# Attention units with sums on VectorE, four probability buffers and longer lags, in a four-layer fused kernel

## What is computed

```python
# layer 0: relative positions, head size 64, values of size 16
content = einsum('bind,bjnd->bnij', q + r_w_bias * SCALE, k)
pos = rel_shift_gather(einsum('bind,tnd->bnit', q + r_r_bias * SCALE, r_head), s, shift=1)
prob = softmax(content + pos, axis=-1)
# layer 1: head size 16, values of size 16
attn = softmax(einsum('bqhd,bkhd->bhqk', q, k) * scale, axis=-1)
# layer 2: head size 64, values of size 64
attn = softmax(einsum('bhnd,bhmd->bhnm', q, k) / SCALE, axis=-1)
# each: attn @ v, then a projection to 192 features, added to the residual
```

## Time and profile before

| | |
|---|---|
| median of three runs | 2116.0 us (2085.26, 2116.0, 2117.72) |
| profiled execution | 2114.3 us, of which the span from first to last instruction is 2112.6 us |
| mean granted TensorE clock | 0.787 of 2.4 GHz |
| TensorE, busy | 1645.4 us (78% of the span) |
| weight loads (PEld), beside it | 1202.3 us (57%) |
| ScalarE, busy | 706.5 us (33%) |
| VectorE, busy | 687.7 us (33%) |
| GpSimd, busy | 382.9 us (18%) |

### The profile page before, as it was taken

How to read it: one execution, slowest core, us unless ns; L and a number is a source line. 1 busy time by engine, 2 the same in 40 slices (tenths; PEclk the granted TensorE clock), 3 DMA queues, 4 the chain that set the end, 5 groups by cost and what they waited for, 6 DMA issues and landing times.

```text
span 2112.6 us, 31289 instructions
## 1 busy us (share of the span) xinstructions
PE 1645.4 (78%) x9952; PEld 1202.3 (57%) x9952; DVE 687.7 (33%) x2153; ACT 706.5 (33%) x2243; POOL 382.9 (18%) x450
## 2 busy tenths in 40 slices
PE   6888788875544557777878869958987899869994
PEld 4565656554322334555556758836656676668883
DVE  1233324245111116634343342224334323451112
ACT  0555454541100003366664201124445443203331
POOL 4111101011000002222220015512112100012331
PEclk9566656565677776888899759979899999858997
DMA  6122222223699983000000425420000020124553
GB/s 179 48 67 57 57 57 57 57 57 90 168 279 286 286 260 97 1 1 0 0 0 0 112 70 167 149 55 1 0 0 0 0 90 0 32 74 124 156 152 83
DMA packets 85963, 177.80 MB, mean 84 GB/s; under 512 B 34602, under 2 KB 53200, under 8 KB 83832
## 3 DMA queue, kind: packets, MB, share of 16 engines
q1 hardware_dynamic: 71344, 127.50, 21.9%
q10 hardware_dynamic: 7392, 33.03, 5.3%
q0 software_dynamic: 7136, 16.10, 2.6%
HBM read 149.61 MB, written 26.99 MB: 84 GB/s over the span
## 4 chain that ended last, share of the span: by engine, by line
PE 46%; issue 22%; DMA 17%; DVE 6%; ACT 5%; POOL 3%; SPq 1%; POOLq 0%; DVEq 0%; ACTq 0%
PE bank L1538 13%; DMA AREA<-in_fc 9%; PE bank L1968 5%; PE bank L1956 5%; PE bank L1715 4%; PE bank L1958 3%; PE bank L1707 3%; DMA pos_scratch<-AREA 3%; DMA AREA<-pos_scratch 2%; PE bank L1638 2%; PE bank L1769 2%; PE bank L1625 2%; PE bank L1648 1%; PE bank L1924 1%; DMA WM<-rows_out 1%
## 5 line engine op out<-in xcount | busy, mean ns | idle before, releaser
L1538 PE MATMUL bank<-XT,AREA 96*128 96x408 f32 (+1 forms) x640 | 244.9, 542 | 32.3 <-ACT XT L1320 15.0
L1538 PEld LDWEIGHTS bank<-XT,AREA 96*128 96x128 f32 (+1 forms) x640 | 124.5, 200 | 142.3 <-issue 103.4
L1625 PE MATMUL bank<-KZ,QT 128*102 128x102 f32 x1152 | 176.0, 305 | 20.6 <-ACT PB L1360 17.9
L609 POOL TENSOR_TENSOR PB<-PB,RCU 102x306 f32<-102x306 f32 x132 | 91.9, 696 | 534.3 <-DVE RCU L843 534.3
L1625 PEld LDWEIGHTS bank<-KZ,QT 128*102 128x102 f32 x1152 | 160.1, 219 | 31.7 <-ACT PB L1360 20.3
L1638 PE MATMUL bank<-PT,V 102*32 102x102 f32 (+1 forms) x1152 | 98.0, 302 | 82.2 <-ACT PT L1366 81.8
L595 POOL TENSOR_TENSOR RS<-VE,expo 102x4 f32<-102x4 f32 (+1 forms) x53 | 53.0, 1000 | 430.3 <-DVE VE L781 372.5
L1360 ACT ACTIVATE PB<-bank,NMU 102x102 f32<-102x102 f32 x264 | 88.0, 346 | 98.5 <-DVE NMU L837 97.5
L1968 PE MATMUL bank<-WM,KZ 128*128 x660 | 120.8, 332 | 0.0
L1956 PE MATMUL bank<-KZ,SLOTS 128*128 128x128 f32 x660 | 116.2, 301 | 2.5 <-issue 2.5
L1638 PEld LDWEIGHTS bank<-PT,V 102*32 102x32 f32 (+1 forms) x1152 | 48.2, 130 | 117.6 <-ACT PT L1366 61.7
(11 more groups left out here) (292 smaller groups left out, 2761.3 us busy)
## 6 DMA issues: line engine op xcount, KB each, us to landing
WM<-in_fc SPq DMA_DIRECT2D x9, 2304.0 KB, 22.4
AREA<-in_fc SPq DMA_DIRECT2D x9, 2304.0 KB, 17.9
WM<-in_fc ACTq DMA_DIRECT2D x7, 2304.0 KB, 29.2
AREA<-in_fc ACTq DMA_DIRECT2D x7, 2304.0 KB, 29.0
pos_scratch<-AREA SPq DMA_DIRECT2D x16, 913.5 KB
SLOTS<-in_m3w SPq DMA_DIRECT2D x33, 384.0 KB
SLOTS<-in_m1w SPq DMA_DIRECT2D x33, 256.0 KB
AREA<-pos_scratch SPq DMA_DIRECT2D x16, 459.0 KB
```

Of the source, the lines that this page charges most:

```text
L609: pool.tensor_tensor(p, p, scale, ALU.mult).then_inc(sem["probs_ready"], 1)
L1538: last = pe.matmul(dst, lhsT, rhs, start=n == 0, stop=n == len(pieces) - 1)
L1625: last = pe.matmul(psum[k][0:T, cols(j)], q, kk, start=True, stop=True)
```

## The change

- **Sums on VectorE.** The exponentials no longer use the accumulator; VectorE reduces each unit's exponentials from PB into SMU, ahead of the reciprocal.
- **Sign and scale in Q's copy.** ScalarE's copies of Q (and QR) are scaled by -0.125 or -0.25, and their biases are scaled once beforehand, so the scores arrive negative and scaled. VectorE takes the minimum and gives it as the exponential's bias, with scale -1; the instruction that multiplied the maxima (L837) goes.
- **Four buffers.** PB has a fourth buffer (in ON0), and MXU, SMU and RCU four places.
- **Banks.** In layers 1 and 2 the scores have three banks and the values two; in layer 0 two and one, as before. Banks of scores and values are freed through exp_ready and a new semaphore pair, values_ready and values_taken.
- **Lags on TensorE.** Turns are three steps behind the scores (before: two), values five (three). A projection comes in three parts in three steps, the first six steps after the batch row's last unit plus one, and is ahead of the values in its step; at the end all three parts stand in the last step.
- **Order on VectorE and ScalarE.** VectorE's copy of the values and the residual addition now stand behind the minimum and the sum of their step. ScalarE's copy of the turned unit (now s-4) stands ahead of the exponentials.
- **Positions in layer 0.** PR exists twice. The six pairs of batch row 2 are made two at a time in steps 0, 1 and 2, those of row 3 in steps 4, 5 and 6.

The core of the diff:

```diff
+POS_STEPS = (0, 1, 2, 4, 5, 6)
-        PB.append(ON[1][:, 0:4 * T].rearrange("p (h t) -> p h t", h=4))
+        for j in (1, 0):
+            PB.append(ON[j][:, 0:4 * T].rearrange("p (h t) -> p h t", h=4))
-        PR = a0(T, HEADS, NREL)
+        PR = [a0(T, HEADS, NREL),
+              SLOTS[0:T, NB * D:NB * D + HEADS * NREL].rearrange("p (h n) -> p h n", h=HEADS)]
-        STEPS = UNITS + 5
-        AVBANK, PROJBANK = OBANKS
+        STEPS = UNITS + 7
+        PROJBANK = OBANKS[1]
+        SCORES, VALUES = (SBANKS + XBANKS[:1], SBANKS), (OBANKS[:1] + XBANKS[1:], OBANKS[:1])
+        def proj_step(bb, i):
+            return min(UPB * bb + UPB + 6 + i, STEPS - 1)
# VectorE
-                step(dve.tensor_reduce(MX[:, 0:HPU], scores, AX.X, ALU.max))
-                give(ts(NMU[:, n % 3, 0:HPU], MX[:, 0:HPU], -scale, None, ALU.mult), "probs_in")
+                give(dve.tensor_reduce(MXU[:, n % 4, 0:HPU], scores, AX.X, ALU.min), "probs_in")
             def inverse_sums(n):
                 dve.wait_ge(sem["exp_ready"], at.take("exp_ready"))
-                give(dve.reciprocal(RCU[:, n % 3, 0:HPU], SMU[:, n % 3, 0:HPU]), "sums_ready")
+                step(dve.tensor_reduce(SMU[:, n % 4, 0:HPU], PB[n % 4][:, 0:HPU, :], AX.X, ALU.add))
+                give(dve.reciprocal(RCU[:, n % 4, 0:HPU], SMU[:, n % 4, 0:HPU]), "sums_ready")
+            def attention(dv, pos, finish):
+                for s in range(STEPS + 1):
                     if s < UNITS:
+                        minima(s, pos)
                     if 0 <= s - 1 < UNITS:
                         inverse_sums(s - 1)
+                    n = s - 6
+                    if 0 <= n < UNITS and av_filled(dv, n % UPB):
+                        tile, k = 3 * av_place(dv, HPU * (n % UPB))[3], VALUES[pos][fill_of(dv, n) % len(VALUES[pos])]
+                        dve.wait_ge(sem["values_ready"], at.take("values_ready"))
+                        src = psum[k][:, 0:3 * T].rearrange("p (k t) -> p k t", k=3)
+                        give(dve.tensor_copy(OT[n // UPB % 2][:, tile:tile + 3, :], src), "values_taken")
+                        dve.wait_ge(sem["values_taken"], at.now("values_taken"))
+                    for bb in range(GB):
+                        if s - 1 == proj_step(bb, 2):
+                            finish(bb, full(PROJBANK)[0:T, 0:D], PROJBANK)
# ScalarE
+                for s in range(UNITS + 4):
+                    if 0 <= s - 4 < UNITS:
                         k = at.bank(TBANKS)
                         src = full(k)[0:T, 0:TU].rearrange("p (h t) -> p h t", h=HPU)
                         free(activation(PT[s % 2][:, 0:HPU, :], src, ACT.Copy), k)
-                            last = activation(p, p if pos else psum[k][0:T, cols(j)], ACT.Exp, scale=scale,
-                                              bias=NMU[:, s % 3, j:j + 1], accum_out=SMU[:, s % 3, j:j + 1])
+                            last = activation(p, p if pos else psum[k][0:T, cols(j)], ACT.Exp, scale=-1.0,
+                                              bias=MXU[:, s % 4, j:j + 1])
-                    activation(QT[:, p, :], src, ACT.Identity, bias=rw0[:, p:p + 1])
-                    free(activation(QR[:, p, :], src, ACT.Identity, bias=rr0[:, p:p + 1]), k)
+                    activation(QT[:, p, :], src, ACT.Identity, scale=-0.125, bias=rw0[:, p:p + 1])
+                    free(activation(QR[:, p, :], src, ACT.Identity, scale=-0.125, bias=rr0[:, p:p + 1]), k)
# TensorE
-                        k = at.bank(SBANKS)
-                        if s < 2:
+                        k = banks[s % len(banks)]
+                        if s < len(banks):
+                    for bb in range(GB):
+                        for i in range(3):
+                            if s != proj_step(bb, i):
+                                continue
+                            if i == 0:
+                                taken(fills(dv) * (bb + 1) - 1)
+                                k, p = claim(None, PROJBANK)
+                            for m in range(i * parts // 3, (i + 1) * parts // 3):
+                                last = pe.matmul(psum[PROJBANK][0:T, 0:D], OT[bb % 2][:, m, :], wo[:, m, :],
+                                                 start=m == 0, stop=m == parts - 1)
-                    n = s - 3
+                    n = s - 5
-                            claim(None, AVBANK)
+                        if f >= len(places) and (unit == 0 or av_filled(dv, unit - 1)):
+                            taken(f - len(places))
-                    n = s - 2
+                    n = s - 3
-                    if pos and s in (UPB, 2 * UPB):
-                        pos(2 if s == UPB else 3)
+                    if pos and s in POS_STEPS:
+                        pos(2 + POS_STEPS.index(s) // 3, 2 * (POS_STEPS.index(s) % 3), 2)
```

More of the change, by code:

```diff
@@ L940, in _ @@
             dve.wait_ge(sem["w0_loaded"], W0_LOADS)
+            for w in (rw0, rr0):
+                give(ts(w, w, -0.125, None, ALU.mult), "scaled")
             def prepare_a0(g):
@@ L1060, in attend_1 @@
                 values(V, 16, bv1)
-                attention(16, False, 0.25, lambda bb, o, k: free(tt(a_of(g)(bb), a_of(g)(bb), o, ALU.add), k))
+                attention(16, False, lambda bb, o, k: free(tt(a_of(g)(bb), a_of(g)(bb), o, ALU.add), k))
             def prepare_f1(g):
@@ L1246, in attend_2 @@
                 values(V, 64, None)
-                attention(64, False, 0.125, lambda bb, o, k: free(tt(h_of(g)(bb), h_of(g)(bb), o, ALU.add), k))
+                attention(64, False, lambda bb, o, k: free(tt(h_of(g)(bb), h_of(g)(bb), o, ALU.add), k))
             def mlp_2(g):
@@ L1351, in exponentials, with attention @@
                 give(activation(buf, buf, ACT.Exp, scale=scale), name)
-            def attention(scale, pos=None):
-                for s in range(STEPS):
-                    if s < UNITS:
-                        k = at.bank(SBANKS)
-                        act.wait_ge(sem["probs_in"], at.take("probs_in"))
-                        for j in range(HPU):
-                            p = PB[s % 3][:, j, :]
-                            last = activation(p, p if pos else psum[k][0:T, cols(j)], ACT.Exp, scale=scale,
-                                              bias=NMU[:, s % 3, j:j + 1], accum_out=SMU[:, s % 3, j:j + 1])
-                        give(last, "exp_ready")
-                    if 0 <= s - 2 < UNITS:
+            def attention(pos=None):
+                for s in range(UNITS + 4):
+                    if 0 <= s - 4 < UNITS:
                         k = at.bank(TBANKS)
@@ L1454, in _ @@
                     k = at.bank(XBANKS)
-                    free(activation(QT[:, dst, :], full(k)[:, 0:TG], ACT.Identity, bias=bqk1[:, dst:dst + 1]), k)
+                    free(activation(QT[:, dst, :], full(k)[:, 0:TG], ACT.Identity, scale=-0.25,
+                                    bias=bqk1[:, dst:dst + 1]), k)
                 for j in range(3):
@@ L1484, in _ @@
                     k = at.bank(XBANKS)
-                    free(activation(QT[:, p, :], full(k)[:, 0:TG], ACT.Copy), k)
+                    free(activation(QT[:, p, :], full(k)[:, 0:TG], ACT.Copy, scale=-0.125), k)
                 for p in range(6):
@@ L1606, in mlp, with attention, taken @@
                     filled(last, k)
-            def attention(dk, per_tile, dv, wo, v_moved, pos=None, whole=False):
-                pt_moved, o_moved = {}, {}
+            def attention(per_tile, dv, wo, v_moved, pos=None):
+                pt_moved = {}
+                banks, places = SCORES[bool(pos)], VALUES[bool(pos)]
+                before = at.now("values_taken")
+                parts = 3 if dv == 16 else 6
+                def taken(f):
+                    pe.wait_ge(sem["values_taken"], before + f + 1)
                 for s in range(STEPS):
@@ L1637, in attention @@
                             row, rows, tile, _ = av_place(dv, h)
-                            last = pe.matmul(psum[AVBANK][row:row + rows, cols(tile)],
+                            last = pe.matmul(psum[k][row:row + rows, cols(tile)],
                                              by_head(dv)[:, bb * HEADS + h, :], PT[n % 2][:, j, :],
@@ L1647, in attention @@
                         for j in range(HPU):
-                            last = pe.transpose(p[0:T, cols(j)], PB[n % 3][:, j, :], ident[0:T, 0:T])
+                            last = pe.transpose(p[0:T, cols(j)], PB[n % 4][:, j, :], ident[0:T, 0:T])
                         pt_moved[n] = filled(last, k)
-                    if pos and s in (UPB, 2 * UPB):
-                        pos(2 if s == UPB else 3)
-                    bb = last_of(s - 4)
-                    if bb is not None:
-                        moved(o_moved[bb])
-                        k, p = claim(None, PROJBANK)
-                        filled(product(p[0:T, 0:D], [(OT[bb % 2][:, n, :], wo[:, n, :])
```

(10 more changed lines are left out.)

92 lines of the change are left out of this document (47 added, 45 removed).

## The result

The median of four executions fell from 2116.9 to 1974.3 us: a ratio of 0.9375, with a 95% interval of 0.9329 to 0.942. The prediction was 1997 us in a range of 1955 to 2060, so it held, and the time forecast was 23 us too high. The profiled execution took 1975.6 us (span 1973.8); the span is 138.8 us shorter.

The account below looks back on a forecast made before the run. Waits between engines, none full, were taken to bound the attention stretches, with TensorE's half clock costing most in layer 0. Layer sums -51, -30 and -36 gave -117 from 2114.3: 1997 us, range 1955 to 2060.

Parts of the forecast that it names:

- Layers 1 and 2: Attention stretches: TensorE's steady waits go, pace 1.25 and 1.44; -30 (bounds -23, -37) and -36 us (-27, -45).
- The wait for VectorE's copy ahead of a projection: TensorE waits for a copy queued behind minimum and sum: 0.7 us in layer 1, 0.5 in layer 2, two times.
- Half the stretches at half clock: Layers 1 and 2: half the stretches lose time to half clock, 3.5 us each in layer 1, 4.4 in layer 2.
- rival 1: All stretches: the clock holds at 2.4 GHz since TensorE has fewer gaps; -63 - 37 - 45, 1969 us; chance 0.17.
- Rivals 3 and 4: 3: VectorE serialises, 2118 us, chance 0.08. 4: TensorE stays at 1.2 GHz in layers 1 and 2, 2209, 0.05.
- Layer 0: Attention stretches: positions spread over steps, VectorE then paces at 1.73; 63.7 to 51 us each, -51 (bounds -63, -27).
- the wait of the values for the one value bank: Layer 0: TensorE's values idle about 2.4 us per batch row behind VectorE's later copy; two waits cost 4.0 before unit 15.
- SyncE's floor: Layer 0: position store 5.66 and load 4.69, 10.4 us per batch row; rows land at 11.4, 21.8, 32.2.
- Rival 2: Layer 0 gives nothing: value-bank wait, SyncE's chain and half clock eat the smoothed position blocks; 2048 us; chance 0.15.
- The accumulators: ScalarE: three accumulator reads go, -0.28 us per unit, a gain only in chains; keeps ScalarE from pacing layer 1 at 1.47.

Follow-up runs that it names:

- the fill in layers 1 and 2: The kernel before, with six extra float32 matmuls (results unused) after the scores of step 1 in layers 1 and 2; ratio 0.9899.
- position blocks: The kernel after, with the positions of batch rows 2 and 3 again as one block each, two PR kept; ratio 0.9637.
- the one with both edits: The kernel after, with VectorE's copy of the values first in its step and the sums back in ScalarE's accumulator; 1925.8 us, ratio 0.9169.

## Why the prediction was right, step by step

**Layers 1 and 2 (forecast -30 and -36, measured -29.3 and -36.2): the sums are right by two errors against each other.** The steady pace is exactly the floors of the earlier trace rows, 1.25 and 1.44, and the turns' wait in the head came as forecast (first turns 3.81 us after the first scores, 890.20 to 894.01; forecast 3.8). Two terms were mis-sized.
- *The wait for VectorE's copy ahead of a projection* was 0.7 in layer 1 and 0.5 in layer 2, and measured 1.42 (step of 3.00 against 1.58) and 1.2 (3.25 against 2.09). The term assumed that VectorE stands at the same step as TensorE. It runs a unit behind: its minimum at 901.90 is of the scores that started at 900.62, when those of 901.87 were already running, and sum, reciprocal and a gap put the copy 1.3 us behind that minimum. The second of the two waits, as long (steps of 3.03 and 3.36), was for the residual addition behind the copy, which the term did not hold. So unit 15's scores started at 22.1 and 25.0 us, not at 20.6 and 23.6, and the tails were 9.0 and 11.9 against 8.3 and 10.9: stretches of 31.1 and 36.9 against 28.9 and 34.5 at full clock.
- *Half the stretches at half clock* (+3.5 and +4.4 in them) did not happen; all ran at 1.00, as rival 1 said. That is 7 and 9 us too much in a layer, and the longer waits and tails were 8 and 9 too little (123.6 against 4 x 28.9, 146.9 against 4 x 34.5).

Rival 1's mechanism thus came true in these layers without its time, since its own sum held the same 0.7 and the same tails. That the layer sums fit to a microsecond is luck. Rivals 3 and 4 did not occur: the sum on VectorE found its exponentials done in nearly every step (0.5 and 0.6 us idle ahead of 16 sums), and no clock fell. The rule of the Trainium skill ("VectorE: DVE Perf Modes", Rules for kernel authors) that tensor_reduce is the slowest VectorE operation is not borne out in the duration: the sum took 0.47 us like the minimum, 0.51 from start to start. Its advice to restructure where it is on the hot path fits all the same: taking it off brought 1.4%.

**Layer 0 (forecast -51, measured -54.7): right, and the position edit is the reason, as given.** How a block costs was told in part. The prediction laid its 6.5 us to ScalarE copying two banks in turn. In the block of the earlier trace rows ScalarE's first copy started only at 114.26, behind exponentials that waited until the positions of batch row 1 had landed (VectorE idle for 3.02 us up to 111.63); that wait was in no term. And the sum took the clock as full from unit 7 on, without saying that most of the gain would then be TensorE's own work at the higher clock (three quarters by the windows). Spread, the positions came as foretold with the copies of ScalarE at their side; the wait of the values for the one value bank appeared three times in each group:

```profile
375.23 0.56 PE L1680 MATMUL bank<-PT,V 102*32 102x102 f32 x6 [3.19 <-DVE OT L868]
...
386.35 0.38 PE L1680 MATMUL bank<-PT,V 102*32 102x102 f32 x6 [2.52 <-DVE OT L868]
...
393.76 0.38 PE L1680 MATMUL bank<-PT,V 102*32 102x102 f32 x6 [0.95 <-DVE OT L868]
```

The first was 3.19 where 2.4 was said, because VectorE lies further behind in layer 0 too, and the scores behind it, at 376.26, ran at half level (1.25 us). In return the clock was full from about unit 2 of the stretch (the scores at 187.64 took 0.78 us), where the sum had half level up to unit 7. SyncE's floor was put at 10.4 a batch row. Its loads in the last group start 8.8 and 9.2 apart, since the next store starts before the load has landed, and the positions of batch row 2 landed 20.3 us into the stretch from 350.9 (forecast 21.8), a moment after VectorE asked for them, as its timeline shows:

```profile
371.23 0.48 DVE L840 TENSOR_TENSOR PB<-bank,AREA 102x306 f32<-102x306 f32 x1 [0.26 <-DMA AREA<-pos_scratch]
```

Rival 2 fell.

**Sign and scale in Q's copy.** Forecast: one VectorE instruction less, 0.20 a unit. It was not tried by itself. The two kernels with ScalarE's sums differ from before in layer 0, beyond the positions, by this, the lags, the order and the buffers, and lie 4 to 5 us under the one with the positions alone (195.9).

**The accumulators (forecast: a gain of 0.28 a unit in chains, and a cover against ScalarE's pace of 1.47).** This is the step that failed. Back on ScalarE the sums pace the steps at 1.30, not 1.47: the 23.6 us that were divided by sixteen hold a table load of 1.3 us, which is no part of a unit, and, at the end of each burst, a latency that instructions without a gap between them hide. Against 0.05 a step stands what the sum cost VectorE: 0.51 in front of every copy, and 1.2 against 0.3 us of waiting for the probabilities in the turns of a stretch of layer 1. With the long lags of this kernel the trade of engines went the wrong way, and the prediction saw the rule against it and set it aside for its size. It moved the sign of no total, because the rest was over four times as large.

**What the sum did not hold: the parts between the groups.** Only the stretches were summed. The 8.6 us between the groups of layer 1 are the clock's (0.81 to 1.00 with the same instructions), carried over from a full stretch. In layer 0 they are 10.6 us shorter too (windows, one such part, before and after):

```profile
261.10:299.70 38.60, 35.63 (x97) 19.95 (x96) 11.31 (x35) 20.06 (x38) 2.01 (x2) 0.50 0.15 39
```

```profile
233.40:267.00 33.60, 29.87 (x99) 16.46 (x96) 11.32 (x35) 19.62 (x38) 2.01 (x2) 0.66 0.17 44
```

That these 10.6 us belong to the change is not shown: in the run that left layer 0 untouched (the fill in layers 1 and 2) they took 97.7 in all, against 111.3 in the profile of the kernel before, and in the other kernels between 84.4 (position blocks) and 105.0, single ones 27 to 39 us as the clock stood. Nor are the 2.1 us ahead of the first stretch the change's: it took 100.3 and 98.2 in the two profiles compared, and 88.9 to 91.1 in all ten others, whatever the kernel. With them these parts are nearly all of the 21.8 us by which the sum was too small (117 forecast, 138.8 measured in the span).

## What to carry to other kernels

Ask of a reordered engine not only what it does per unit but which instruction of its queue another engine waits for, and put that one first: here the copy of the values, behind a minimum and a sum, cost 1%. Work that occupies one engine in a block while its drain stands in another engine's queue (the positions) can cost more than its own time: the block waits, the scores behind it wait, and here TensorE's clock was lower as well; spreading it over the steps, from an earlier step on, took 59 us off layer 0. And sum over what follows a stretch as well: a clock that holds is worth something in the code behind, which was not edited.

## What was not expected of the hardware

- Six matmuls of 102 x 128 by 102 without any use, in an idle time of step 1, kept TensorE at 2.4 GHz through all of layer 1 of the kernel before and took 1% off the whole (ratio 0.9899, 0.9849 to 0.995). In layer 0, 46 extra matmuls a group raised the clock from 0.64 to 0.81 and lost 1.3%.
- A matmul over 128 rows put between the pairs of position matmuls (64 rows each) kept neighbouring pairs from running together: 0.94 us for two pairs without it, 0.93 for one pair with it.
- At a unit pitch of 1.25 us the accumulator reads of three exponentials cost 0.05 us a unit, though their records are 0.24 to 0.26 us each in the mean and ScalarE's busy time rises from 19.9 to 22.8 us in a stretch of layer 1 (the kernel after and the one with both edits).
